# Upper products of an image as eight 64x32 tiles, and final products as four 64x64 tiles

## The chip, the cores and the metric

One core of one Trainium2 chip runs the kernel. The metric is the device time of one execution in microseconds. The five engines named below are TensorE (PE; its weight loads are listed as PEld), VectorE (DVE), ScalarE (ACT), GpSimd (POOL) and SyncE (SP), which only starts DMAs here.

## The reference, cut to what matters

The input x is 8 images of 64 channels on a grid of 16x16 points, fp32. Two layers follow each other, each with a group norm ahead of it and a residual sum behind it.

```python
x = x + local_attention(_gn(x), ...)        # 3x3 mean, q/k/v, 9 taps, 8 heads, gate, projection
x = x + relu(deformable_conv(_gn(x), ...))  # 64 -> 64 channels, 3x3 taps, 4 groups of 16 channels
```

The second layer takes most of the time. A 3x3 convolution gives for each point, tap (9) and group (4) an offset (dy, dx) and a mask. For each tap the image is sampled bilinearly at the shifted point, multiplied by the mask, and the 9x64 sampled values are multiplied by `w_dcn` and summed. A bilinear sample is a sum over rows and columns of the image, weighted by "hats" max(0, 1-|distance|) in y and in x. The kernel writes it as matrix products: weights made of image rows, times moving data made of the product of a y hat and an x hat. A weight matrix for one image and a pair of rows has 128 rows (2 image rows x 4 groups x 16 columns) and 64 columns (the channels), and is zero where the group of the row isn't the group of the channel.

## The kernel before

**Stages.** The attention layer runs until about 54 us. Then come the second norm, the offset convolution (`convolve`, in five pieces; pieces 3 and 4 are computed later, inside the sampling loop), the split of its results into three bf16 parts that go to `stack` by DMA, and from about 75 us the sampling loop `sampling(0)`. It has 72 steps: image i (0 to 7) and tap m (0 to 8). Every engine has its own order of work, written out by hand as a loop over the same steps, and semaphores tie the engines together. A second pass exists for far offsets (`it` not an int); it isn't run with these inputs.

**One step on TensorE** (`sampling` under `block.tensor`), in this order: `spread_y` of the next tap (6 matmuls of 256 columns, fp16, banks 0 to 3 in turn); on every second step `select_x` (4 matmuls, bank 5); a part of the products; a part of `convolve` in images 0 and 3; `select_y` (steps 1, 3, 7) and `spread_mask` (table `MASKS`), both to bank 7; `windows`; and in step `FINAL` the final products of the image before.

**The products.** PSUM holds for each image and each of three tap rows ki and two sides (halves of the image) a 64 x 384 block. The table `BLOCKS` puts two of them at a time in steps 6, 7 and 8, `LATE` in steps 0, 1 and 2 of the next image: kind 0 is ki 0 and 1 of side 0 in bank 4, kind 1 the same of side 1 in bank 6, kind 2 is ki 2 of both sides in bank 4. Each pair is two tiles of 128 rows x 64 columns. A tile takes up to 6 matmuls over row pairs, with 96, 192, 288, 288, 192, 96 moving columns; fp32 matmuls appear as two MATMUL records each. Kind 0 has no matmul for the row pair outside the image.

**One step on VectorE**: `multiply` (rows times x hat, PSUM to `smp`, L852); `values` (products times mask, L866) in steps 8, 1 and 3; `accumulate` and `finish` (L874, L879, L885) in step FINAL+1; then in this order `window_out` for odd window groups (L837), `offset_part` and `stage`.

**The windows.** `windows(g)` transposes four 128x128 blocks of image rows to PSUM (L1129, one record per transpose); ACT copies the even groups out, DVE the odd ones. There are 17 groups: three ahead of the loop, six in steps 0 to 5 of image 0, four each in steps 2 to 5 of images 1 and 2. Group g+1 waits for the copy of g where steps 3 and 5 say so.

**The final products** (`final`, in step 5 for the image before): 3 matmuls of 256 columns with `wa` and 6 of 128 columns with `wb`, all of 128 rows x 64 columns, into the two halves of bank 6. `accumulate` adds the two halves.

**At the start** ACT builds a permutation `by_tap`, PE multiplies it with the weights (`wfin`, L981 to L983), ACT copies pieces of the result to `wa` and `wb` (L495 to L502), and PE runs two filler products (`keep_warm(2)`, L976) before it multiplies q, k and v.

Of the kernel before, what the change touches and what calls it, by code (L numbers as in the profile page):

```python
# [5 lines left out]
B, C, H, W = 8, 64, 16, 16  # L6
HW = H * W
HALVES = 2
# [4 lines left out]
TAPS = 9  # L13
# [41 lines left out]
DX = DG * W  # L55

# [26 lines left out]
CHUNK, VALS, SLICES = 3, 3, 6  # L83
SEL_Y = {1: 0, 3: 1, 7: 2}
BLOCKS = {6: (0, 0), 7: (0, 1), 8: (1, 0)}
LATE = {0: (1, 1), 1: (2, 0), 2: (2, 1)}
FINAL = 5
# [7 lines left out]
def seventh(i, m):  # L95

    at = i * STEPS + m - 1
    while at >= 0:
        i, m = divmod(at, STEPS)
        if m in SEL_Y and i + 1 < B:  # L100
            return "y", 3 * (i + 1) + SEL_Y[m] + 1
        if m in MASKS[i]:
            c, part = MASKS[i][m]
            return "m", SLICES * c + part + 1
        at -= 1
    return "y", 3


def bass_local_attention_then_deformable_conv(nc, x, cf, wom, sel16, rows16, out):
# [8 lines left out]
    with ExitStack() as ctx:  # L118
# [24 lines left out]
        wa = sb("wa", [P, 3 * C])  # L143
        wb = sb("wb", [P, 6 * C])
# [119 lines left out]
        def mask_of(i, part):  # L264
# [3 lines left out]
            if part < 2:  # L268
                m = masks[:, at:at + 3 * BANK].rearrange("p (k i n) -> p k i n", k=3, i=2)[:, :, side_, part * HF:(part + 1) * HF]
# [9 lines left out]
        s_perm, s_wtap, s_wzero, s_wfin = sem("s_perm"), sem("s_wtap"), sem("s_wzero"), sem("s_wfin")  # L279
# [60 lines left out]
        def _(sp):  # L340
# [4 lines left out]
            sp.dma_start(selx[:, :].bitcast(u16), sel16["selx"]).then_inc(s_selxd, 16)  # L345
# [40 lines left out]
        def _(pool):  # L386
# [5 lines left out]
            nc.gpsimd.memset(wb[:, :], 0.0).then_inc(s_wzero, 1)  # L392
# [31 lines left out]
            pool.wait_ge(s_byd, 16)  # L424
            for a in range(2):
                src = bcast[:, 0:2 * DG * P].rearrange("p (d a r x) -> p a r d x", d=DG, a=2, r=WROWS)[:, a, 0:ROWS]
                dst = by_rows[:, a * QUARTERS * P:(a + 1) * QUARTERS * P].rearrange("p (r d x) -> p r d x", r=ROWS, d=DG)
                nc.gpsimd.tensor_copy(dst, src).then_inc(s_byrows, 1)
# [8 lines left out]
            def stage(j, shift):  # L437

                rows = images(tall)[:, j, bass.ds(shift * (ROWS * W), SROWS * W)].rearrange("p (r x) -> p r x", r=SROWS)
                nc.gpsimd.tensor_tensor(staged_image(j), rows.unsqueeze(2).to_broadcast([P, SROWS, DG, W]), group_mask(SROWS),  # L440
                                        ALU.mult).then_inc(s_staged, 1)
# [37 lines left out]
        def _(act):  # L479
# [9 lines left out]
            act.wait_ge(s_wzero, 1)  # L489
            lower, upper = slice(0, C), slice(C, P)  # L490
            straight = bank(1)[:, 0:PAIRS * C].rearrange("p (k o) -> p k o", o=C)
            swapped = bank(2)[:, 0:PAIRS * C].rearrange("p (k o) -> p k o", o=C)
            wa3 = wa[:, :].rearrange("p (k o) -> p k o", o=C)
            wb3 = wb[:, :].rearrange("p (k h o) -> p k h o", k=3, h=2)
            nc.scalar.copy(wa3[lower, 0:3:2], straight[lower, 0:2]).then_inc(s_wfin, 1)  # L495
            nc.scalar.copy(wa3[lower, 1], swapped[lower, 0]).then_inc(s_wfin, 1)
            nc.scalar.copy(wa3[upper, 0:3:2], straight[upper, 1:3]).then_inc(s_wfin, 1)
            nc.scalar.copy(wa3[upper, 1], swapped[upper, 2]).then_inc(s_wfin, 1)
            nc.scalar.copy(wb3[lower, 0:3:2, 0], straight[lower, 3:5]).then_inc(s_wfin, 1)
            nc.scalar.copy(wb3[lower, 1, 0], swapped[lower, 3]).then_inc(s_wfin, 1)  # L500
            nc.scalar.copy(wb3[upper, 0:3:2, 1], swapped[upper, 3:5]).then_inc(s_wfin, 1)
# [991 lines left out]
```

## Time and profile before

| what | value |
|---|---|
| median of 3 runs | 208.38 us (208.22 to 208.55) |
| the profiled execution's own time | 208.33 us |
| its span in the trace | 206.5 us |
| PE busy / DVE busy / ACT busy / POOL busy | 182.0 / 159.5 / 106.4 / 86.7 us |
| granted TensorE clock, mean | 0.999 |

The span is the time from the first to the last recorded instruction; the 1.8 us between it and the profiled time lie around it. A busy time is the union of an engine's instructions. PE records carry a modelled end which includes the way through the array, so starts of consecutive matmuls are a better measure than durations.

### The profile page before, as it was taken

The numbers are of one execution on the slowest core, as the hardware profiler recorded it, in microseconds if no ns is written. First come the engines' busy times: TensorE is split into PE (matmuls) and PEld (weight loads), VectorE is DVE, ScalarE is ACT, GpSimd is POOL, SyncE is SP. The second block draws the span as 40 slices with busy tenths as digits, with TensorE's granted clock in tenths as the row PEclk, the third lists the DMA queues.
The fourth block names the chain that finished last, engine by engine and source line by source line (L and its number), as shares of the span: only waits on it lengthen the run. The fifth ranks groups of instructions, "written<-read, shape, count | busy, mean of one in ns | idle before, by whom it ended". The sixth has DMA issues, their size and how long they took to land.

```text
span 206.5 us, 4572 instructions
## 1 busy us (share of the span) xinstructions
PE 182.0 (88%) x1808; PEld 127.9 (62%) x1808; DVE 159.5 (77%) x257; ACT 106.4 (51%) x199; POOL 86.7 (42%) x104
## 2 busy tenths in 40 slices
PE   0399996989989989999979999999969999998980
PEld 0224963644357535468668879639958789877870
DVE  0479958994869769888889779816999798899922
ACT  0325238500006795678748657836766687864000
POOL 8523982666013086504354343340561654442000
PEclk9999999999999999999999999999999999999999
DMA  6940000000040010010011000000002100000000
GB/s 193 325 28 0 3 0 2 3 0 0 0 102 14 25 30 9 17 43 3 7 29 33 0 3 0 3 0 0 12 25 62 28 0 16 2 16 2 19 0 21
DMA packets 8499, 5.54 MB, mean 27 GB/s; under 512 B 4887, under 2 KB 7461, under 8 KB 8473
## 3 DMA queue, kind: packets, MB, share of 16 engines
q1 hardware_dynamic: 8089, 4.25, 7.9%
q10 hardware_dynamic: 288, 0.89, 1.3%
q8 instruction: 16, 0.26, 0.5%
q14 instruction: 10, 0.08, 0.1%
q0 software_dynamic: 96, 0.06, 0.1%
HBM read 2.82 MB, written 0.52 MB: 16 GB/s over the span
## 4 chain that ended last, share of the span: by engine, by line
PE 67%; DVE 15%; ACT 6%; issue 4%; DMA 3%; POOL 2%; SPq 0%; DVEq 0%; ACTq 0%; POOLq 0%
PE ps L1218 20%; PE ps L1192 10%; PE ps L1112 10%; PE ps L1008 4%; PE ps L1129 3%; DVE smp_prod L742 3%; DMA x_parts<-in_x 3%; PE ps L1260 3%; PE ps L1266 3%; PE ps L1045 3%; PE ps L1177 2%; PE ps L991 2%; PE ps L1163 2%; DVE smp_prod L852 2%; PE ps L1146 2%
## 5 line engine op out<-in xcount | busy, mean ns | idle before, releaser
L852 DVE TENSOR_TENSOR smp_prod<-ps,hx_selx 128x768 f32<-128x768 f32 x72 | 67.5, 953 | 10.1 <-PE ps L1192 8.8
L1218 PE MATMUL ps<-smp_prod,windows_attention 128*64 128x192 f32 (+2 forms) x512 | 54.9, 336 | 0.0
L1218 PEld LDWEIGHTS ps<-smp_prod,windows_attention 128*64 128x64 f32 x512 | 40.1, 136 | 4.1 <-ACT windows_attention L574 0.3
L1192 PE MATMUL ps<-haty,by_rows 128*64 128x256 f16 x432 | 39.4, 275 | 2.0 <-DVE smp_prod L852 1.8
L450 POOL TENSOR_SCALAR disty<-disty 64x512 f32<-64x512 f32 (+1 forms) x23 | 13.5, 586 | 64.4 <-ACT haty L595 64.3
L1192 PEld LDWEIGHTS ps<-haty,by_rows 128*64 128x64 f16 x432 | 26.1, 109 | 9.7 <-DVE smp_prod L852 3.9
L603 ACT ACTIVATE hx_selx<-ps 128x512 f32<-128x512 f32 x36 | 21.3, 591 | 10.8 <-PE ps L1177 10.7
L457 POOL TENSOR_TENSOR haty<-disty,haty 64x512 f16<-64x512 f32 (+1 forms) x23 | 24.0, 1042 | 1.9
L1112 PE MATMUL ps<-conv_staged 128*108 128x512 f32 (+1 forms) x60 | 23.3, 521 | 0.7 <-ACT x_parts L567 0.7
L605 ACT ACTIVATE hx_selx<-hx_selx 128x512 f32<-128x512 f32 x36 | 22.7, 630 | 1.1
L590 ACT ACTIVATE disty<-ps 128x512 f32<-128x512 f32 (+1 forms) x24 | 12.5, 521 | 12.3 <-PE ps L1163 12.3
L581 ACT COPY windows_attention<-ps 128x512 f32<-128x512 f32 (+1 forms) x24 | 11.3, 473 | 10.7 <-PE ps L1146 9.5
L866 DVE TENSOR_TENSOR vals_attw<-ps,windows_attention 128x384 f32<-128x384 f32 x24 | 13.3, 554 | 4.1 <-PE ps L1218 3.4
L1177 PE MATMUL ps<-stack_x,selx 110*64 110x256 bf16 x144 | 15.6, 272 | 0.0
L453 POOL TENSOR_SCALAR disty<-disty 64x512 f32<-64x512 f32 (+1 forms) x23 | 14.8, 643 | 1.9
L1112 PEld LDWEIGHTS ps<-conv_staged 128*108 128x108 f32 x60 | 9.5, 172 | 8.0 <-issue 6.0
L595 ACT ACTIVATE haty<-disty 128x512 f16<-128x512 f32 (+1 forms) x24 | 13.4, 559 | 0.8
L567 ACT ACTIVATE x_parts<-ps,kept 108x256 f32<-108x256 f32 (+1 forms) x3 | 1.6, 540 | 22.1 <-PE ps L1112 22.0
L421 POOL TENSOR_TENSOR smp_prod<-smp_prod 128x1024 f32<-128x1024 f32 x4 | 9.3, 2358 | 6.0 <-DVE smp_prod L742 6.0
L1045 PE MATMUL ps<-smp_prod,kept 128*128 128x512 f32 x20 | 9.6, 611 | 1.6 <-POOL smp_prod L421 1.6
L742 DVE TENSOR_TENSOR smp_prod<-ps,windows_attention 128x1024 f32<-128x1024 f32 x9 | 10.5, 1212 | 0.1
L1163 PE MATMUL ps<-stack_y,s_sely 110*64 110x256 bf16 x80 | 9.4, 278 | 1.0 <-ACT windows_attention L581 0.7
(137 smaller groups left out, 273.9 us busy)
## 6 DMA issues: line engine op xcount, KB each, us to landing
x_parts<-in_x SPq DMA_DIRECT2D x2, 256.0 KB, 5.3
bcast<-in_bcast SPq DMA_DIRECT2D x2, 256.0 KB, 6.7
x2seq<-x_parts SPq DMA_DIRECT2D x2, 256.0 KB, 3.7
out<-x_parts SPq DMA_DIRECT2D x8, 64.0 KB, 2.2
vals_attw<-in_cf ACTq DMA_DIRECT2D x1, 480.0 KB, 5.8
stack_m<-x_parts SPq DMA_DIRECT2D x12, 36.0 KB
kept<-in_cf ACTq DMA_DIRECT2D x1, 390.5 KB, 4.5
conv_staged<-in_wom SPq DMA_DIRECT2D x1, 324.0 KB, 6.9
```

The costliest lines, as they stand in the source:

```text
L453: nc.gpsimd.tensor_scalar(d, d, -1.0, 1.0, ALU.add, ALU.mult).then_inc(s_uy, 1)
L457: nc.gpsimd.tensor_tensor(hi, d, hi, ALU.add).then_inc(s_loy, 1)
L603: nc.scalar.activation(h, bank(5), ACT.Abs).then_inc(s_absx, 1)
L605: nc.scalar.activation(h, h, ACT.Relu, bias=1.0, scale=-1.0).then_inc(s_hatx, 1)
L742: nc.vector.tensor_tensor(grid(prod[:, t * N:(t + 1) * N]), grid(bank(PB[pos % 3], 2)), shifted(vpad, t), ALU.mult).then_inc(s_pv, 1)
L852: nc.vector.tensor_tensor(pairs, rows, cols.unsqueeze(1).to_broadcast([P, QUARTERS, HW]), ALU.mult).then_inc(s_mult, 1)
L1045: ins = nc.tensor.matmul(bank(2 + c), ident, prod[:, t * N + c * BANK:][:, 0:BANK], start=(t == 0), stop=(t == 6))
L1112: ins = nc.tensor.matmul(bank(CONV_BANK[p])[0:OM, lo:hi], womt[:, k * OM:(k + 1) * OM], shifted(dup[h], 3 * ky + 2 * single)[:, j:j + (hi ...
L1163: ins = nc.tensor.matmul(bank(7)[h * C:(h + 1) * C, k * HW:(k + 1) * HW], sely[:, p * P + h * C:p * P + (h + 1) * C], stack["y"][:, i * HW ...
L1177: ins = nc.tensor.matmul(bank(5)[h * C:(h + 1) * C, k * HW:(k + 1) * HW], selx[:, tap * P + h * C:tap * P + (h + 1) * C], stack["x"][:, i ...
L1192: ins = nc.tensor.matmul(ps[h * C:(h + 1) * C, at:at + HW], by_matrix(a, QUARTERS - 1 - k)[:, h * C:(h + 1) * C], haty[i % 2][:, p * HW:(p ...
L1218: return nc.tensor.matmul(dst[:, at:at + strips * 3 * SP].rearrange("p (s k n) -> p s k n", k=3, n=SP), rows, sampled(i, ki, m, first, str ...
```

## The change

The 128 rows of the weights are put in another order, so that the first 64 partitions hold groups 0 and 1 and the last 64 groups 2 and 3 (e = 0, 1). A matrix for ki 0 or 1 then splits in two dense blocks of 64 rows x 32 columns. All eight (2 ki, 2 sides, 2 e) are issued interleaved, in steps 6 and 7 (`UPPER`), e = 0 to bank 4 and e = 1 to bank 6. Steps 8 and 0 have no products; ki 2 stays two tiles of 128x64, in steps 1 and 2 (`LOWER`). Masks of ki 0 and 1 come as eight 110x32 matmuls of 256 columns in place of two 110x64 of 512. Window transposes become eight matmuls of 128x64 with the identity. The final products become 18 matmuls of 64x64 and 128 columns, on four tiles, side 0 in bank 6 and side 1 in bank 7, and move from step 5 to step 4; `accumulate` moves from step 6 to 5. `values` part 1 moves from step 1 to 0. The x and y hats, staging and weights are laid out to match. Cut to its core:

```diff
-CHUNK, VALS, SLICES = 3, 3, 6
+CHUNK, VALS, SLICES = 2, 3, 6
-BLOCKS = {6: (0, 0), 7: (0, 1), 8: (1, 0)}
-LATE = {0: (1, 1), 1: (2, 0), 2: (2, 1)}
-FINAL = 5
+UPPER = {6: 0, 7: 1}
+LOWER = {1: 0, 2: 1}
+FINAL = 4
+EIGHTH = C // 2
...
-            sp.dma_start(selx[:, :].bitcast(u16), sel16["selx"]).then_inc(s_selxd, 16)
+            for r in range(2):
+                sp.dma_start(selx[:, :].bitcast(u16).rearrange("p (t e r c) -> p r t e c", t=TAPS, e=2, r=2)[:, r],
+                             sel16["selx"].rearrange("p (t r e c) -> p r t e c", t=TAPS, e=2, r=2)[:, r]).then_inc(s_selxd, 16)
...
-                    if (i, m) == (0, 6) and isinstance(it, int):
+                    if (i, m) == (0, 5) and isinstance(it, int):
                         offsets(3)
...
-                    if m == 1 and i:
+                    if m == 0 and i:
                         values(i - 1, 1, it)
...
-            nc.tensor.matmul(bank(1)[:, 0:PAIRS * C], by_tap[:, :], cst["wfin"], start=True, stop=True)
-            nc.tensor.matmul(bank(2)[0:C, 0:PAIRS * C], by_tap[:, C:P], cst["wfin"], start=True, stop=True)
-            nc.tensor.matmul(bank(2)[C:P, 0:PAIRS * C], by_tap[:, 0:C], cst["wfin"], start=True, stop=True).then_inc(s_wtap, 1)
+            for a in range(2):
+                for e in range(2):
+                    for u in range(4):
+                        nc.tensor.matmul(bank(1 + a)[u * EIGHTH:(u + 1) * EIGHTH, e * 3 * C:(e + 1) * 3 * C],
+                                         by_tap[:, a * C + e * EIGHTH:a * C + (e + 1) * EIGHTH], cst["wfin"][:, 0:3 * C],
+                                         start=True, stop=True)
+                for side in range(2):
+                    ins = nc.tensor.matmul(bank(0)[side * C:(side + 1) * C, a * 2 * C:(a + 1) * 2 * C],
+                                           by_tap[:, a * C:(a + 1) * C], cst["wfin"][:, 3 * C:5 * C], start=True, stop=True)
+            ins.then_inc(s_wtap, 1)
...
-                    ins = nc.tensor.transpose(bank(dst)[:, k * P:(k + 1) * P], rows, ident)
+                    for e in range(2):
...
+                        ins = nc.tensor.matmul(bank(dst)[e * C:(e + 1) * C, k * P:(k + 1) * P], rows, ident, start=True,
+                                               stop=True)
...
-                    for h in range(HALVES):
-                        ins = nc.tensor.matmul(bank(7)[h * C:(h + 1) * C], selm[:, k * P + h * C:k * P + (h + 1) * C], src,
-                                               start=True, stop=True)
+                    for e in range(2):
+                        for u in range(4):
+                            side, ki = divmod(u, 2)
+                            at = k * P + ki * C + e * EIGHTH
+                            ins = nc.tensor.matmul(bank(7)[u * EIGHTH:(u + 1) * EIGHTH, e * HW:(e + 1) * HW],
+                                                   selm[:, at:at + EIGHTH], sides[:, side], start=True, stop=True)
...
+            def upper_products(i, part, it):
+                if part == 0:
+                    reach(pe, s_mult, STEPS * i + 6, it)
+                    reach(pe, s_vals, VALS * i, it)
+                    reach(pe, s_acc, i, it)
+                    settled(pe, it)
+                products(i, [(ki, side, e, bank(6 if e else 4)[(2 * side + ki) * EIGHTH:(2 * side + ki + 1) * EIGHTH])
+                             for side in range(2) for ki in range(2) for e in range(2)], part, it)
...
             def final(i, it):
                 reach(pe, s_vals, VALS * (i + 1), it)
+                bank7_free(i + 1, FINAL if i + 1 < B else 0, it)
+                settled(pe, it)
+                def term(side, g, n, start, stop):
+                    rows = slice(side * C, (side + 1) * C)
+                    e, kj = divmod(n, 3)
+                    w = (wu[rows, n * C:(n + 1) * C] if e < 2 else wl[rows, kj * C:(kj + 1) * C])
+                    src = vals[rows, e * 6 * C:(e + 1) * 6 * C].rearrange("p (s k n) -> p k s n", k=3, n=SP)[:, kj]
+                    dst = bank(6 + side)[g * C:(g + 1) * C, 0:HF].rearrange("p (s n) -> p s n", n=SP)
+                    return nc.tensor.matmul(dst, w, src, start=start, stop=stop, skip_group_check=True)
+                for n in range(5):
+                    for side in range(2):
+                        if n < 4:
+                            term(side, 1, 5 + n, n == 0, n == 3)
+                        ins = term(side, 0, n, n == 0, n == 4)
+                ins.then_inc(s_fin, 1)
...
-                    if i == 0 and m < TAPSTEPS and isinstance(it, int):
+                    if i == 0 and m < 5 and isinstance(it, int):
                         if m == 0:
                             pe.wait_ge(s_omraw, 3)
-                        convolve(3, m)
+                        for n in (m,) if m < 4 else (4, 5):
+                            convolve(3, n)
```

Also in the diff: `stage` writes each image in two instructions (one per e) in place of one, `by_rows` is copied in four instructions in place of two, ACT makes 10 copies of the weights in place of 8, POOL no longer clears `wb`, `farthest` moves on DVE from step 4 to 3 of image 5, and PE waits for `s_omraw` 4 in step 6 of image 0 in place of 8.

## Rows read from the trace of the kernel before

**Rows 1.** The page: busy times, and the chain that ended last, by engine
```profile
PE 182.0 (88%) x1808; PEld 127.9 (62%) x1808; DVE 159.5 (77%) x257; ACT 106.4 (51%) x199; POOL 86.7 (42%) x104
PE 67%; DVE 15%; ACT 6%; issue 4%; DMA 3%; POOL 2%; SPq 0%; DVEq 0%; ACTq 0%; POOLq 0%
```
**Rows 2.** Busy time by stretch: stretch, length, PE, PEld, DVE, ACT, POOL, clock, DMA
```profile
76.00:90.20 14.20, 14.15 (x96) 6.92 (x96) 11.29 (x16) 8.67 (x16) 8.12 (x10) 1.00 0.07 19
90.20:99.20 9.00, 8.98 (x117) 7.00 (x117) 7.95 (x10) 7.80 (x15) 2.73 (x4) 1.00 0.04 11
...
106.80:116.30 9.50, 9.48 (x125) 8.05 (x121) 8.45 (x13) 6.79 (x13) 3.00 (x5) 1.00 0.09 26
...
123.10:133.30 10.20, 10.07 (x138) 8.53 (x133) 8.86 (x12) 7.89 (x16) 3.87 (x6) 1.00 0.01 2
...
141.30:155.40 14.10, 12.53 (x176) 10.97 (x173) 13.75 (x21) 9.34 (x18) 6.59 (x9) 1.00 0.06 16
155.40:168.10 12.70, 12.57 (x172) 10.44 (x170) 11.42 (x21) 9.50 (x18) 4.38 (x7) 1.00 0.13 34
...
180.80:192.90 12.10, 11.31 (x158) 9.72 (x155) 11.31 (x16) 6.03 (x10) 3.72 (x5) 1.00 0.03 8
```
**Rows 3.** Groups of instructions by line and form: busy us, mean ns
```profile
L852 DVE TENSOR_TENSOR smp_prod<-ps,hx_selx 128x768 f32<-128x768 f32 x72 | 67.5, 953 | 10.1 <-PE ps L1192 8.8 <-DVE x_parts L813 0.4
L866 DVE TENSOR_TENSOR vals_attw<-ps,windows_attention 128x384 f32<-128x384 f32 x24 | 13.3, 554 | 4.1 <-PE ps L1218 3.4 <-ACT windows_attention L581 0.5
```
**Rows 4.** Timeline of PE, one part of kind 2: start, length, what
```profile
171.21 1.19 PE L1218 MATMUL ps<-smp_prod,windows_attention 128*64 128x96 f32 x12
172.18 0.33 PE L1152 MATMUL ps<-stack_m,s_selm 110*64 110x256 bf16 x2
```
**Rows 5.** Attention logits, 32-column tiles: matmuls in flight in 20 ns; the chain
```profile
22.90:22.92 0.02, 0.02 (x4) 1.00 0.00 0
23.85:23.87 0.02, 0.02 (x8) 1.00 0.00 0
...
20.37 7.61 PE ps L1008 x144
```
**Rows 6.** Timeline of PE in image 0, step 1 to 2 of the loop
```profile
80.18 0.39 PE L1177 MATMUL ps<-stack_x,selx 110*64 110x256 bf16 x4
80.49 1.11 PE L1112 MATMUL ps<-conv_staged 128*108 128x512 f32 x2
81.44 0.60 PE L1129 MATMUL ps<-kept,smp_prod 128*128 128x128 f32 x4
81.97 0.52 PE L1192 MATMUL ps<-haty,by_rows 128*64 128x256 f16 x6
```
**Rows 7.** Timeline of PE at the start of the kernel
```profile
11.81 3.48 PE L976 MATMUL ps<-kept 128*128 128x512 f32 x4
15.70 1.10 PE L991 MATMUL ps<-windows_attention,vals_attw 128*128 128x512 f32 x2 [0.41 <-DVE windows_attention L703]
```
**Rows 8.** Timeline of ACT and PE ahead of the loop
```profile
71.37 0.60 ACT L590 ACTIVATE disty<-ps 128x512 f32<-128x512 f32 x1
...
76.04 1.11 PE L1112 MATMUL ps<-conv_staged 128*108 128x512 f32 x2 [0.67 <-ACT x_parts L567]
```
**Rows 9.** Timeline of image 2, steps 4 to 6
```profile
118.91 0.66 PE L1129 MATMUL ps<-kept,x_parts 128*128 128x128 f32 x4
...
119.68 0.68 DVE L837 COPY windows_attention<-ps 128x512 f32<-128x512 f32 x1
...
120.41 0.66 PE L1129 MATMUL ps<-kept,x_parts 128*128 128x128 f32 x4 [0.40 <-DVE windows_attention L837]
...
122.61 0.42 DVE L874 COPY x_parts<-ps 64x256 f32<-64x256 f32 x1 [1.38 <-PE ps L1266]
...
122.90 1.03 PE L1218 MATMUL ps<-smp_prod,windows_attention 128*64 128x192 f32 x8
```
**Rows 10.** Timeline of the last image
```profile
199.08 0.56 DVE L866 TENSOR_TENSOR vals_attw<-ps,windows_attention 128x384 f32<-128x384 f32 x1 [1.39 <-PE ps L1218]
199.69 0.86 PE L1260 MATMUL ps<-vals_attw,wa 128*64 128x256 f32 x5 [0.65 <-DVE vals_attw L866]
201.30 0.42 DVE L874 COPY x_parts<-ps 64x256 f32<-64x256 f32 x1 [1.66 <-PE ps L1266]
```

More of the change, by code:

```diff
@@ L488, in _ @@
             act.wait_ge(s_wtap, 1)
[L489 to L501, printed above, removed]
[L502 removed]
+            wu4 = wu[:, :].rearrange("p (e k o) -> p e k o", e=2, o=C)
+            wl3 = wl[:, :].rearrange("p (k o) -> p k o", o=C)
+            last = bank(0)[:, 0:4 * C].rearrange("p (a k o) -> p a k o", a=2, o=C)
+            for a in range(2):
+                taps = bank(1 + a)[:, 0:6 * C].rearrange("p (e k o) -> p e k o", e=2, o=C)
+                for side in range(2):
+                    for ki in range(2):
+                        rows = slice((2 * side + ki) * EIGHTH, (2 * side + ki + 1) * EIGHTH)
+                        if ki == a:
+                            nc.scalar.copy(wu4[rows, :, 0:3:2], taps[rows, :, a:a + 2]).then_inc(s_wfin, 1)
+                        else:
+                            nc.scalar.copy(wu4[rows, :, 1], taps[rows, :, 2 * ki]).then_inc(s_wfin, 1)
+            nc.scalar.copy(wl3[:, 0:3:2], last[:, 0]).then_inc(s_wfin, 1)
+            nc.scalar.copy(wl3[:, 1], last[:, 1, 0]).then_inc(s_wfin, 1)
             def out_of_q(c):
@@ L1224, in needed, with products @@
                         if not isinstance(it, int) or pair_of_rows(i, ki, m)[1]]
-            def products(i, tiles, dst, part, it):
-                lists = [needed(i, ki, side, it) for ki, side in tiles]
+            def products(i, tiles, part, it):
+                lists = [needed(i, ki, side, it) for ki, side, _, _ in tiles]
                 for m in range(part * 3, part * 3 + 3):
-                    for n, (ki, side) in enumerate(tiles):
+                    for n, (ki, side, e, dst) in enumerate(tiles):
@@ L1251, in final, with lower_products @@
+            def lower_products(i, part, it):
+                if part == 0:
+                    reach(pe, s_mult, STEPS * (i + 1), it)
+                    reach(pe, s_vals, VALS * i + 1, it)
+                products(i, [(2, side, None, bank(4)[side * C:(side + 1) * C]) for side in range(2)], part, it)
             def final(i, it):
                 reach(pe, s_vals, VALS * (i + 1), it)
-                both = vals[:, 0:12 * C].rearrange("p (s k n) -> p k s n", k=3, n=SP)
-                lower = vals[:, 12 * C:18 * C].rearrange("p (s k n) -> p k s n", k=3, n=SP)
@@ L1256, in final @@
-                out_ = [bank(6)[h * C:(h + 1) * C, 0:HW] for h in range(2)]
-                def upper(h, kj, start):
-                    return nc.tensor.matmul(out_[h].rearrange("p (s n) -> p s n", s=STRIPS), wa[:, kj * C:(kj + 1) * C],
-                                            both[:, kj], start=start, stop=False, skip_group_check=True)
-                def below(h, kj, top, stop=False):
-                    at = (2 * kj + top) * C
-                    return nc.tensor.matmul(out_[h][:, top * HF:(top + 1) * HF].rearrange("p (s n) -> p s n", n=SP),
-                                            wb[:, at:at + C], lower[:, kj], start=False, stop=stop, skip_group_check=True)
@@ L1335, in sampling @@
                         final(i - 1, it)
-                for m in range(3):
-                    block_of_products(B - 1, *LATE[m], it)
+                for part in range(2):
+                    lower_products(B - 1, part, it)
                 final(B - 1, it)
```

137 lines of the change are left out of this document (65 added, 72 removed).

## The prediction

> **What bounds the kernel now.** I read the page first, then the busy times by stretch, then timelines of one step each. On the page PE is the busiest engine and two thirds of the chain that ended last, with DVE second [rows 1]. That is an average over stages, so the table of stretches decides. The reader is to see three regimes in it [rows 2]. From 76 to 133 us, images 0 to 2, PE is busy for nearly the whole of each stretch shown (14.15 of 14.20, 8.98 of 9.00): time taken from or added to PE there moves the end. In image 3 to 4 (141.3 to 155.4) DVE has 13.75 of 14.10: a faster PE brings little. In the last images both are close: 12.57 PE and 11.42 DVE of 12.70, at the end 11.31 and 11.31 of 12.10. DVE's own work per image is 9 multiplies and 3 values, 9 x 0.953 + 3 x 0.554 = 10.2 us [rows 3], and about 1.3 for accumulate and finish (three of 0.42 to 0.5, one of them in rows 9). That is 11.6 us, a floor which the change doesn't touch.
>
> **Upper products.** Two tiles with 96+192+288 columns each, in two records per matmul (12 in all), take 172.18 - 171.21 = 0.97 us [rows 4], so a record costs 0.97/1152 = 0.84 ns per column with both tiles at once, at the granted clock of 1.00 (2.4 GHz). A full tile (1152 columns, two records) is 1.94 us, kind 0 with a strip less 1.77. The change puts kinds 0 and 1, 3.71 us, on eight tiles at once: 1.94 us if the array sets the pace. It issues 84 records. Eight tiles appear nowhere. The nearest rows are the 32-column tiles of the logits: 4 records are in flight with two tiles active and 8 where two calls with other tiles overlap [rows 5], so twice as many tiles do carry twice the work there, and the pace is 27 ns a record, half of 7.61/144 = 53 ns. 84 x 27 = 2.27 us. Bounds: 1.94 and 84 x 53 = 4.45. I take 2.1, near the row with most tiles: a gain of 1.6 us an image for PE.
>
> **Changes of tile shape.** Between a 64-column and a 128-column shape PE loses time: L1177 to L1112 is 0.31 us where two rounds of 256 bf16 columns take 0.21 (0.42 ns a column, half of fp32's); L1112 to L1129 is 0.95 for 2 x 512 x 0.84 = 0.86, by a first weight load of 128 columns; L1129 to L1192 is 0.53 for four transposes that need 0.44 [rows 6]. So about 0.1 us lies in each gap, and some more in the first weight load behind it: I use 0.12 towards the narrower shape, 0.18 towards 128 columns. The change brings new ones: four an image for the upper products (two where a mask follows joins them), two for final, two for each mask slice of ki 0 and 1, some nine in all, or 1.1 us an image. The Trainium skill, "TensorEngine Tiling (Array Packing)", Key Properties, says that a change of tiling mode, not of tile, drains TensorE, which speaks against this change; by that rule the price applies to all nine, and rows 6 agree for the one pair that they show. Bounds from rows: 0 (a kind not shown) and 0.18.
>
> **Windows.** Four transposes are 0.44 us [rows 6]. Eight fp32 matmuls of 128 columns on two tiles are 16 records x 128 x 0.84/2 = 0.86: +0.42 each, 17 times. Where no convolution stands beside them the two changes to 128 columns (0.30) go, which leaves +0.12.
>
> **The sum, by place.** The list adds to the profiled execution's 208.33 us, which is the median's within 0.05.
> 1. Start. The weight products grow from 6 records of 320 columns to 24. They run at half rate: four records of 512 columns take 3.48 [rows 7], 0.85 each against 0.43 (512 x 0.84) later. Four rounds of 192 columns (0.32 each) and two of 128 (0.21), twice, with four changes, end some 1.4 us later than now. Fillers follow and end near 15.3; q/k/v wait until 15.70 for DVE, so 0.4 of it is hidden, and part of the fillers falls into the full clock. +0.15.
> 2. Ahead of the loop, windows 0 and 1 stand before the select_y which ACT awaits at 71.37; from there ACT is busy without a gap to 75.99, and PE waits for it until 76.04 [rows 8]. Two times 0.42 and some of a change: +0.95. ACT hid nothing there.
> 3. Image 0, steps 0 to 5, PE-bound [rows 2]: +0.42 in steps 0 and 2, +0.12 in 1 and 3, +0.24 in 4, +0.06 in 5, where a convolution piece leaves and takes its two changes with it: +1.4.
> 4. Products of images 0, 1, 2 (90.2 to 133.3, three stretches of rows 2): -1.6 each, +0.48 for their changes, +0.12, 0.6, 0.24 for masks, less about 0.2 idle that goes. DVE's 7.95 of 9.00 is the next limit in the first. -0.9 -0.7 -0.75 = -2.35.
> 5. Steps 4 to 6 of images 1 and 2. Window group 16 waits for DVE's copy of 15, which now follows multiply 5 at once [rows 9]. After the change final stands in step 4 and accumulate and finish in step 5 ahead of that copy, so the chain is window 15 (0.86), final (1.25), accumulate and finish (1.35 with the way to DVE), copy (0.68), window 16 (0.86), ACT's copy (0.6, so far beside final), upper. From window 15 at 118.91 to the product at 122.90 are 4.0 us now; the chain has 5.6 and some 0.3 of waits and a change, and window groups 13 and 14 add 0.8 before it. +2.6; in image 1 DVE has other work there which already held PE: +1.8. What queues behind PE's wait is spread_y for tap 7, so DVE waits as well.
> 6. Image 3 to 4, DVE-bound; accumulate and finish now fall in the convolution gap ahead: -0.5.
> 7. Images 4 to 6 (37.5 us): upper part 0 starts when accumulate is done; DVE then has finish, multiplies 6, 7, 8 (3.3 us) against PE's two parts, changes and spread_y (3.3). So DVE is the bound, 11.6 and 0.2 of gaps each, +0.3 for farthest in image 5: 35.7. -1.8.
> 8. End. From values part 2 to accumulate 1.66 [rows 10] becomes 1.5, and lower products start at values part 0: -0.3.
> Sum: 0.15 + 0.95 + 1.4 - 2.35 + 4.4 - 0.5 - 1.8 - 0.3 = +1.95, so **210.3 us**. The rest costs nothing by its cover: the split DMA of selx (needed at 68 us, all loads of constants are done by 15), four copies on POOL for two (POOL waits 8.7 us behind them), ACT's weight copies (needed by 20 us), two stage instructions for one (+0.1, DVE waits there).
>
> **Rivals.** (B) Faster: the new shape changes cost nothing, since only 64 to 128 columns is shown. Against: it is the same engine and the same gap. Nine an image in stretches 4 (-2.0), two in step 5 (-0.5), the end and item 1 (-0.6), and 8-tile products at 1.94 (-0.4): 206.8. It decides below about 0.06 us a change. If the copy chain of item 5 also costs half, 205.
> (C) Eight tiles don't pay: records go no faster than 53 ns over a long run [rows 5], 4.45 us an image, 2.35 above my value in all eight: PE is then the bound everywhere, 210.3 + 8 x 2.1 = 227; at 40 ns, 3.4 us, about 216. For: no row has row tiles. Against: 8 in flight. The Trainium skill, "TensorE: Matmul & The Clock Gate", Part 1, names some 62 ns per MATMUL without hardware decode; by an estimate from that page 84 would take 5.2 us, but rows 4 and 5 show shorter paces in bursts, so I give it little.
> (D) PE gains but DVE and ACT are late everywhere, no net change: 208.4.
>
> **Chances.** Forecast 0.50, C 0.11, B 0.33, D 0.06. Less than 0.2% (0.42 us) can't be told from no change here. Slower 0.61, same 0.06, faster 0.33. The range 205.2 to 214.8 holds B with half of the chain, and C only up to some 35 ns a record; the forecast's own range is 208.8 to 212.5 (change price 0.08 to 0.15, chain 3 to 5).
>
> **What would show it.** Upper records: 40 in step 6, spanning 1.0 to 1.1 us start to start (right), 2 or more (C). Gaps at upper and final of about 0.1 beyond column time (B: none). L1129's successor: 0.86 per group. The wait of PE for L837 in images 1 and 2: over 2 us each against 0.40 now. L852's idle in the last images near zero, period 11.8. Wrong if the loop starts no later than now or if windows aren't 0.4 longer.

## The result: 220.2 us, 5.6% slower

| | before | after |
|---|---|---|
| median (lowest to highest, 4 runs each) | 208.36 us (208.22 to 208.55) | 220.21 us (219.81 to 220.47) |
| span of the profiled execution | 206.5 us | 217.9 us |
| instructions of PE (matmuls) | 1808 | 2598 |

The ratio is 1.056, 95% interval 1.055 to 1.058. Forecast were 210.3 us and a range of 205.2 to 214.8: slower was right, but of +11.85 us only +1.95 had been seen. Two executions among the experiments (222.45 us in the fourth, 223.56 us in the ninth) were over 1.5% longer than the fastest of their kernel, and the medians and ratios given there leave them out. The page of after, which answers to [rows 1]:

```profile
PE 181.0 (83%) x2598; PEld 117.7 (54%) x2598; DVE 162.2 (74%) x261; ACT 108.1 (50%) x201; POOL 84.9 (39%) x105
PE 55%; DVE 21%; ACT 9%; issue 8%; DMA 3%; POOL 2%; DVEq 0%; SPq 0%; ACTq 0%; POOLq 0%
```

PE works 1.0 us less and the kernel takes 11.4 us more, and the chain that ended last holds less PE and more DVE, ACT and issue. The time lies in waits. To see where, I cut both kernels at the first multiply of each image; the last stretch reaches to the end. Columns as in [rows 2]: stretch, length, PE, PEld, DVE, ACT, POOL, clock, DMA. Before:

```profile
71.92:93.46 21.54, 20.86 (x162) 11.11 (x164) 17.98 (x23) 15.84 (x30) 11.23 (x12) 1.00 0.09 24
...
126.17:144.59 18.42, 18.29 (x189) 12.69 (x187) 11.23 (x16) 12.12 (x23) 6.25 (x9) 1.00 0.00 1
...
158.95:171.62 12.67, 12.54 (x170) 10.46 (x168) 11.39 (x21) 10.05 (x19) 6.52 (x9) 1.00 0.10 24
...
sum 134.58, PE 123.06 PEld 94.19 DVE 106.79 ACT 83.00 POOL 52.24; mean PE 15.38 PEld 11.77 DVE 13.35 ACT 10.38 POOL 6.53
```

After:

```profile
72.42:97.15 24.73, 23.32 (x324) 14.15 (x320) 18.66 (x24) 16.01 (x30) 10.17 (x12) 1.00 0.08 21
97.15:116.55 19.40, 15.48 (x304) 11.81 (x300) 14.93 (x22) 11.71 (x23) 6.23 (x9) 1.00 0.05 15
116.55:134.65 18.10, 15.63 (x310) 11.95 (x310) 12.56 (x17) 10.72 (x21) 6.25 (x9) 1.00 0.03 7
134.65:154.48 19.83, 17.86 (x264) 10.16 (x260) 11.37 (x15) 12.39 (x23) 6.23 (x9) 1.00 0.01 2
154.48:169.45 14.97, 11.84 (x232) 8.30 (x234) 14.71 (x21) 8.84 (x18) 6.82 (x9) 1.00 0.10 28
169.45:184.12 14.67, 12.62 (x252) 8.21 (x248) 12.15 (x19) 10.61 (x20) 6.24 (x9) 1.00 0.08 20
184.12:197.58 13.46, 11.47 (x232) 8.47 (x234) 11.75 (x16) 8.74 (x18) 6.25 (x9) 1.00 0.03 8
197.58:217.90 20.32, 12.83 (x260) 9.31 (x256) 13.09 (x20) 4.35 (x8) 2.39 (x3) 0.91 0.05 11
sum 145.48, PE 121.04 PEld 82.35 DVE 109.21 ACT 83.38 POOL 50.56; mean PE 15.13 PEld 10.29 DVE 13.65 ACT 10.42 POOL 6.32
```

The reader is to take the length less PE's busy time: over the loop it grows from 134.58 - 123.06 = 11.5 us to 145.48 - 121.04 = 24.4. Image 3 had 0.13 us of it and has 1.97, image 5 had 0.13 and has 2.05. No engine is full in images 1, 2, 3, 5 and 6. The table sets the lengths beside the prediction's sum; its items 6 and 7 go by places half an image or more later than these stretches, so its terms are regrouped and the last three rows match only roughly.

| stretch | before | after | change | forecast (items) |
|---|---|---|---|---|
| up to the first multiply | 71.92 | 72.42 | +0.50 | +1.10 (1, 2) |
| image 0 | 21.54 | 24.73 | +3.19 | +0.50 (3, part of 4) |
| image 1 | 17.51 | 19.40 | +1.89 | +1.10 (4, 5) |
| image 2 | 15.20 | 18.10 | +2.90 | +1.85 (4, 5) |
| image 3 | 18.42 | 19.83 | +1.41 | -0.50 (6) |
| images 4 to 6 | 40.13 | 43.10 | +2.97 | -1.80 (7) |
| last image | 21.80 | 20.32 | -1.48 | -0.30 (8) |

The place that item 7 spoke of, image 6, steps 4 to 6, in the timeline of after (start, length, what, idle before it):

```profile
189.25 2.04 DVE L867 TENSOR_TENSOR smp_prod<-ps,hx_selx 128x768 f32<-128x768 f32 x2
...
190.74 0.45 PE L1298 MATMUL ps<-vals_attw,wu 64*64 64x128 f32 x8 [0.23 <-ACT disty L603]
...
192.10 0.42 DVE L888 COPY x_parts<-ps 64x256 f32<-64x256 f32 x1 [0.82 <-PE ps L1298]
192.55 0.43 DVE L893 TENSOR_TENSOR x_parts<-ps,x_parts 64x256 f32<-64x256 f32 x1
193.01 1.17 DVE L899 SCALAR_TENSOR_TENSOR x_parts<-x_parts,x2seq 64x256 f32<-64x256 f32 x1
194.21 2.69 DVE L867 TENSOR_TENSOR smp_prod<-ps,hx_selx 128x768 f32<-128x768 f32 x3
```

Multiplies 4 and 5 run, then DVE waits 0.82 us for final, does accumulate (L888, L893) and finish (L899), and only then multiply 6. Before, the same place reads:

```profile
177.56 2.90 DVE L852 TENSOR_TENSOR smp_prod<-ps,hx_selx 128x768 f32<-128x768 f32 x3
...
178.98 0.81 PE L1260 MATMUL ps<-vals_attw,wa 128*64 128x256 f32 x5
...
180.54 0.42 DVE L874 COPY x_parts<-ps 64x256 f32<-64x256 f32 x1
```

Three multiplies in a row run beside final, and accumulate follows 0.08 us behind them. The forecast had moved accumulate one step ahead at no cost.

### The profile page after: what moved, and what is told of

It is laid out like the page before. It is cut to its first block, busy times and chain, and to the rows that moved or that the text cites. A ratio compares the mean times of both kernels' runs of the same rounds, so it can differ in the third digit from the quotient of the medians.

```text
span 217.9 us, 6167 instructions
## 1 busy us (share of the span) xinstructions
PE 181.0 (83%) x2598; PEld 117.7 (54%) x2598; DVE 162.2 (74%) x261; ACT 108.1 (50%) x201; POOL 84.9 (39%) x105
## 4 chain that ended last, share of the span: by engine, by line
PE 55%; DVE 21%; ACT 9%; issue 8%; DMA 3%; POOL 2%; DVEq 0%; SPq 0%; ACTq 0%; POOLq 0%
PE ps L1249 12%; PE ps L1133 9%; PE ps L1151 6%; PE ps L1219 6%; DVE smp_prod L867 4%; PE ps L1298 4%; PE ps L1029 3%; DVE smp_prod L755 3%; ACT disty L603 3%; DMA x_parts<-in_x 3%; PE ps L1066 3%; PE ps L1190 2%; PE ps L1012 2%; PE ps L1204 2%; DVE x_parts L893 1%
## 5 line engine op out<-in xcount | busy, mean ns | idle before, releaser
L463 POOL TENSOR_SCALAR disty<-disty 64x512 f32<-64x512 f32 (+1 forms) x23 | 13.1, 569 | 80.3 <-ACT haty L608 80.2
L1219 PE MATMUL ps<-haty,by_rows 128*64 128x256 f16 x432 | 36.6, 275 | 4.9 <-DVE smp_prod L867 4.9
L1249 PE MATMUL ps<-smp_prod,windows_attention 64*32 64x192 f32 (+5 forms) x848 | 37.1, 337 | 3.0 <-ACT windows_attention L587 1.1
L1249 PEld LDWEIGHTS ps<-smp_prod,windows_attention 64*32 64x32 f32 (+1 forms) x848 | 23.7, 112 | 10.9 <-issue 3.3
L1219 PEld LDWEIGHTS ps<-haty,by_rows 128*64 128x64 f16 x432 | 22.3, 109 | 13.2 <-DVE smp_prod L867 9.3
L1204 PE MATMUL ps<-stack_x,selx 110*64 110x256 bf16 x144 | 14.3, 273 | 0.0
L466 POOL TENSOR_SCALAR disty<-disty 64x512 f32<-64x512 f32 (+1 forms) x23 | 13.5, 588 | 1.9
L1298 PE MATMUL ps<-vals_attw,wu 64*64 64x128 f32 x192 | 10.6, 277 | 2.4 <-ACT disty L603 1.4
L1298 PEld LDWEIGHTS ps<-vals_attw,wu 64*64 64x64 f32 x192 | 8.7, 132 | 4.7 <-issue 2.8
```

Of the source, the lines that this page charges most:

```text
L466: nc.gpsimd.tensor_scalar(d, d, -1.0, 1.0, ALU.add, ALU.mult).then_inc(s_uy, 1)
L1204: ins = nc.tensor.matmul(bank(5)[h * C:(h + 1) * C, k * HW:(k + 1) * HW], selx[:, tap * P + h * C:tap * P + (h + 1) * C], stack["x"][:, i ...
L1219: ins = nc.tensor.matmul(ps[h * C:(h + 1) * C, at:at + HW], by_matrix(a, QUARTERS - 1 - k)[:, h * C:(h + 1) * C], haty[i % 2][:, p * HW:(p ...
L1249: return nc.tensor.matmul(dst[:, at:at + strips * 3 * SP].rearrange("p (s k n) -> p s k n", k=3, n=SP), rows, sampled(i, ki, m, first, str ...
L1298: return nc.tensor.matmul(dst, w, src, start=start, stop=stop, skip_group_check=True)
```

## Experiments

W is the theory that the loss is waits, that is the order of the work; S that the narrow shapes (windows, changes of shape) cost more than rated. The kernel before was timed beside each group of runs: 208.5 to 208.6 us. After was timed once, for the result above: 220.2 us. The code is shortened to the lines that matter.

**The windows alone, in the kernel before.**

```diff
-ins = nc.tensor.transpose(bank(dst)[:, k * P:(k + 1) * P], rows, ident)
+for e in range(2):
+    ins = nc.tensor.matmul(bank(dst)[e * C:(e + 1) * C, k * P:(k + 1) * P], rows[:, e * C:(e + 1) * C],
+                           ident, start=True, stop=True)
```

> The kernel before with one edit: each of the four transposes of a window group becomes two fp32 matmuls of 64 columns (the form that the change brings), same partition order, same values. It prices the windows alone. Theory W (the 11.85 us are waits: PE work that used to stand between the users of bank 7 and between final and the next multiply is gone) expects only the terms of the prediction: two groups ahead of the loop +0.84, seven in image 0 +1.4, eight in images 1 and 2 at +0.12 to 0.42, so about +3.5, 211.9 us. Theory S (the narrow shapes and their changes cost more than rated) expects at least half of the missing 9.9 us here: 215 us or more.

212.56 us, ratio 1.019 (1.013 to 1.024): +4.0. By stretch, from the trace: the first multiply comes 1.07 us later (forecast for the two groups ahead of the loop: 0.95), image 0 is 1.60 longer (1.4), image 1 0.42, image 2 1.15, and the rest is unchanged to 0.06. W is borne out against S: the windows cost 4.0 us where 3.5 had been expected.

**The windows taken back, in the changed kernel.**

```diff
-for e in range(2):
...
-    ins = nc.tensor.matmul(bank(dst)[e * C:(e + 1) * C, k * P:(k + 1) * P], rows, ident, start=True,
-                           stop=True)
+ins = nc.tensor.transpose(bank(dst)[:, k * P:(k + 1) * P], rows, ident)
```

> The changed kernel with the windows as four whole 128x128 transposes a group, as before. Their rows then lie in another order in the image of windows, so the sampled values are wrong; the rest of the work is the same. Theory W: the mirror of the first run, about -3.5 of 220.2, so 216.7 us. Theory S: -7 or more, 213 us or less.

218.55 us, ratio 1.044 (1.037 to 1.052), lowest run 216.54: -1.7 in the median, less than either theory said. By stretch, image 0 gives back 2.15 us, but image 1 is 1.05 longer than in after. In images 1 and 2 the granted clock was 0.92 and 0.91 in the mean, where after has 1.00:

```profile
94.46:114.91 20.45, 16.05 (x256) 10.89 (x252) 14.93 (x23) 11.82 (x23) 6.23 (x9) 0.92 0.05 15
114.91:133.14 18.23, 16.03 (x262) 10.59 (x262) 12.56 (x17) 10.58 (x21) 6.26 (x9) 0.91 0.02 6
```

By these rows the clock cost up to 0.08 x 20.45 + 0.09 x 18.23 = 3.3 us. With 1.7 that is 5.0, near what the windows cost (4.0 in the kernel before, 4.8 by the run with both causes undone, below). They are not S's cause, and there is a second effect, the clock, taken up below.

**The order.** Final back in step 5, accumulate behind multiply 6, upper products in steps 7 and 8, mask slice of step 6 in step 4.

```diff
-UPPER = {6: 0, 7: 1}
+UPPER = {7: 0, 8: 1}
-FINAL = 4
+FINAL = 5
-         {0: (1, 2), 2: (1, 3), 6: (1, 4), 8: (1, 5)}, {0: (2, 0), 2: (2, 1), 6: (2, 2), 8: (2, 3)},
+         {0: (1, 2), 2: (1, 3), 4: (1, 4), 8: (1, 5)}, {0: (2, 0), 2: (2, 1), 4: (2, 2), 8: (2, 3)},
...
-                    if m == 8:
-                        values(i, 0, it)
                     if m == 0 and i:
+                        values(i - 1, 0, it)
+                    if m == 1 and i:
                         values(i - 1, 1, it)
```

> The changed kernel, same instructions, other steps: final back in step 5 (behind spread_y for tap 6, so that multiply 6 can run beside it) with accumulate behind multiply 6, the upper products in steps 7 and 8, values part 0 and 1 in steps 0 and 1, the mask slice of step 6 in step 4. Theory W: the 5.3 us from multiply 5 to 7 of images 5 and 6 (3.1 and 3.9 before) shorten by some 1.5 an image, and so do those of images 1 to 3; 220.2 - 7 = 213 us. Theory S: the order changes nothing much, 219 to 221 us.

212.13 us, ratio 1.017 (1.011 to 1.024): 8.1 us less than after with the same instructions. This is the main finding. By stretch against after: -0.78 in image 0, -1.98, -1.83, -1.50, -0.93, -0.81 and -1.12 in images 1 to 6, +1.02 at the end. Two rows of its stretches:

```profile
130.17:148.50 18.33, 17.73 (x273) 10.33 (x278) 11.17 (x17) 12.38 (x23) 6.24 (x9) 1.00 0.01 2
...
176.41:188.74 12.33, 11.26 (x240) 8.20 (x229) 11.63 (x17) 9.51 (x19) 6.25 (x9) 1.00 0.04 9
```

In these two PE's busy time is that of after to 0.2 us; what went is idle (image 3: 1.97 to 0.60, image 6: 1.99 to 1.07), and image 6 is now held by DVE, 11.63 of 12.33, 0.8 shorter than before, which is the kind of gain that item 7 had forecast.

**DVE's copies ahead of accumulate.**

```diff
+                    if isinstance(it, int):
+                        if (i, m - 1) in PAIRS_AT:
+                            g, src = PAIRS_AT[i, m - 1]
+                            if g % 2:
+                                window_out(g, it, src)
                     if m == FINAL + 1 and i:
                         accumulate(i - 1, it)
```

> The changed kernel with DVE's copies of window groups in front of accumulate and finish. Only images 1 and 2 have both in step 5. The prediction's item 5 has accumulate and finish (1.35 us and ways) in front of the copy that window groups 12 and 16 wait for; with the copy first it runs beside final, and the first upper product of those images comes some 2.0 us sooner: 220.2 - 3.5 = 216.7 us. If the upper products are held by accumulate anyway (they wait for it too), it is 0.7 us later there and nothing is won: 220 to 221 us.

218.07 us, ratio 1.042 (1.034 to 1.050), lowest run 216.70. Image 1 is 1.43 shorter than in after and image 2 1.92, 3.35 together as expected: the chain of item 5 is real. But in the profiled execution image 3 is 1.7 longer. The trace says why (columns as above, the clock is the last but two):

```profile
132.00:134.00 2.00, 0.63 (x8) 0.36 (x8) 1.97 (x3) 1.97 (x4) 1.21 (x2) 1.00 0.00 0
134.00:136.00 2.00, 1.92 (x24) 1.57 (x26) 0.79 (x1) 0.97 (x3) 1.17 (x2) 0.64 0.00 0
136.00:138.00 2.00, 2.00 (x16) 1.27 (x14) 0.17 (x1) 1.09 (x3) 0.00 (x0) 0.51 0.00 0
138.00:140.00 2.00, 2.00 (x32) 1.35 (x28) 1.51 (x2) 0.98 (x3) 1.15 (x3) 1.00 0.00 0
```

PE had little to do from 132 to 134 and was then granted half its clock (1.2 GHz) for some 3.5 us of full work: 0.36 x 2 + 0.49 x 2 = 1.7 us lost. So a gap in PE can cost more than its length. But it is no new gap that did it. PE's wait ahead of the fall, in this run and then the same wait in after:

```profile
134.08 0.40 PE L1174 MATMUL ps<-stack_m,s_selm 110*32 110x256 bf16 x8 [1.44 <-ACT windows_attention L594]
```

```profile
137.04 0.40 PE L1173 MATMUL ps<-stack_m,s_selm 110*32 110x256 bf16 x8 [1.44 <-ACT windows_attention L594]
```

In after the clock stayed at 1.00 behind it, and behind longer ones (1.48 and 1.70 us) too. In the loop of after the clock is 1.00 in seven stretches; the 0.91 of the last one holds its end, where PE has no work left (0.64 from 213 us on).

**Mask slices on 32-column tiles, in the kernel before.**

```diff
-                    for h in range(HALVES):
...
+                    for half in range(2):
+                        for u in range(4):
```

> The kernel before with each mask slice of ki 0 and 1 (twelve slices, two matmuls of 64x512 columns) written as eight matmuls of 32 output columns and 256 columns, same values: the same column time on the array and two more changes of tile shape a slice. It prices the change of shape, of which the prediction put 0.12 us on each. Nine of the twelve slices lie in images 0 to 3, which PE bounds: +2.1 us by the prediction's price, 210.5; by rival B (shape changes free) 208.4. By theory S (more than rated) 0.25 us a change or more: 213.

Two matmuls of 64 columns by 512 become eight of 32 by 256. 210.43 us, ratio 1.008 (1.004 to 1.013). In step 6 of image 0 the PE timeline of this kernel reads

```profile
90.28 1.03 PE L1221 MATMUL ps<-smp_prod,windows_attention 128*64 128x192 f32 x8
91.24 0.40 PE L1148 MATMUL ps<-stack_m,s_selm 110*32 110x256 bf16 x8
91.57 0.52 PE L1195 MATMUL ps<-haty,by_rows 128*64 128x256 f16 x6
```

From the products to spread_y are 91.57 - 90.28 = 1.29 us, against 91.25 - 90.17 = 1.08 in before (the starts of L1218 and L1192 there): 0.21 for two changes, 0.11 each where 0.12 was taken. Rival B is out. The total near the 210.5 forecast is in part luck: images 0 and 1 became only 0.12 us longer with five slices in them, where the price gives 1.2, and images 4 to 6, left out of the expectation, 0.91. In steps 4 and 5 of image 0 the slice stands between a convolution piece and window transposes, so it has a change on either side in before too: from it to the transposes are 0.34 us there and 0.33 here, and nothing is added. The Trainium skill, "TensorEngine Tiling (Array Packing)", Key Properties, has it that a change of tiling mode drains TensorE; the trace agrees, at 0.11 us a change.

**Finish behind multiply 6.**

```diff
                         accumulate(i - 1, it)
-                        if isinstance(it, int):
+                    if isinstance(it, int):
+                        if m == FINAL + 2 and i:
                             finish(i - 1, 1)
```

> The changed kernel with finish moved behind multiply 6 (step 6), accumulate as it is. In the trace finish stands between accumulate and multiply 6, 0.42 us long, 1.16 in images 5 and 6. If multiply 6 is what the image waits for there (theory W), the copy for groups 12 and 16 and multiply 6 come 0.4 us sooner in images 1 to 4 and 1.2 in 5 and 6: 220.2 - 3.5 = 216.7. If finish only moves and is paid a step later (DVE is the bound), -1 at most: 219.2 or more.

218.33 us, ratio 1.046 (1.039 to 1.053), and its profiled span is 2.5 us shorter than after's: 0.44, 0.45, 0, 0.09, 0.78, 0.93 in images 1 to 6. Between the two expectations; finish was in the way, most where it took 1.16 us, and some is paid a step later.

**Only final in step 5; only the products in 7 and 8.** The two halves of the third run, each alone (the mask slice moves with final).

> The changed kernel with final in step 5, accumulate behind multiply 6 and the mask slice of step 6 in step 4, but the upper products still in steps 6 and 7: one half of the third run. Multiply 6 then runs beside final, but the upper products still wait for accumulate in the step in which it ends, as they hold both banks. Theory W, first half (multiply behind accumulate costs): two thirds of the 8 us, 215 us. W, second half (the products' place costs): PE now waits for accumulate in front of the products, and most of it stays: 218 to 221 us.

221.03 us, ratio 1.056 (1.049 to 1.063).

> The other half of the third run: the changed kernel with the upper products in steps 7 and 8 (values part 0 and 1 in steps 0 and 1 of the next image), but final in step 4 and accumulate and finish ahead of multiply 6 as in the change. The half with final alone won nothing (221.0). If the two halves only work together (the products must not wait for accumulate, and multiply 6 must not wait for final), this half brings under 2 us: 218.5 to 220.5. If the products' place alone was the loss, it brings the 8 us: 212.5.

220.89 us, ratio 1.056 (1.049 to 1.063). Neither half wins anything, both together 8 us. With final alone moved, images 1, 2 and 6 are 1.08, 0.98 and 0.97 shorter than in after, but 3 and 4 are 1.97 and 1.69 longer, where its clock was 0.92 and 0.90:

```profile
133.00:135.00 2.00, 0.65 (x10) 0.36 (x8) 2.00 (x3) 1.94 (x5) 1.06 (x2) 1.00 0.00 0
135.00:137.00 2.00, 1.77 (x28) 1.40 (x30) 1.00 (x2) 1.39 (x4) 1.32 (x2) 0.82 0.00 0
137.00:139.00 2.00, 2.00 (x16) 1.37 (x14) 0.08 (x1) 1.20 (x3) 0.00 (x0) 0.50 0.00 0
```

With the products alone moved, images 0 to 3 are 0.79, 1.54, 0.62 and 1.51 shorter, and 5, 6 and the last 2.4, 1.4 and 2.6 longer, at clocks of 0.90, 0.94 and 0.95. Each half does win in most images where the clock held, and a fall of the clock takes that back (0.10 x 17.1 = 1.7 us of the 2.4 in image 5). With the products alone moved, PE's gaps ahead of the falls are longer than in after (1.79 and 2.16 us); with final alone moved, the first fall follows the same gap of 1.44 us that stands in after. That the halves work only together is so of the times, and the clock is a large part of why; how much of the 8 us each half is worth at a full clock was not measured.

**Upper products over three steps.**

```diff
-UPPER = {6: 0, 7: 1}        # window rows 0-2, 3-5
+UPPER = {6: 0, 7: 1, 8: 2}  # window rows 0-1, 2-3, 4-5
```

> The changed kernel with the same 84 records of upper products over steps 6, 7 and 8 (two window rows each) where the change has 6 and 7. Theory W in the form that PE work must stand between the users of bank 7: 2 us less, 218. If only the place of the start counts (bank 6 and accumulate), no gain, or values part 0 comes later: 220 to 221.

223.55 us, ratio 1.071 (1.066 to 1.076): 3.3 us slower. My form of W by which PE lacked work between the users of bank 7 is wrong. Values part 0 need the last window row, which now comes a step later: in image 5 DVE waits 1.59 us in front of them, where after has 0.27.

**The eighth run's edits.** On the third run's order, finish behind multiply 7 and ACT's reads of bank 7 ahead of its hats; and the same two edits on the kernel before.

```diff
-if t % 2 == 0 and t // 2 + LEAD < UNITS: hat_x(...)
 if m in SEL_Y and i + 1 < B: distance_y(...)
 if m in MASKS[i]: mask_out(...)
+if t % 2 == 0 and t // 2 + LEAD < UNITS: hat_x(...)
```

> The third run's order and two edits more: finish behind multiply 7, and ACT reads bank 7 (distance, masks) ahead of its hats of a step. In the third run PE waits 0.2 to 1.1 us an image for these reads, 1.1 in image 0. Theory W: -1.5, 210.6 us. If DVE bounds the images already: -0.3, 211.8.

210.59 us, ratio 1.009 (1.006 to 1.013): -1.5.

> The kernel before with the two edits that the eighth run added: finish one step later, ACT's reads of bank 7 ahead of its hats. A control: before has PE work beside these reads. Theory W: under 0.6 us less, 208.0 against 208.5; if they help it as much as the third run's order (-1.5), the edits say nothing of the change.

211.04 us, ratio 1.011 (1.007 to 1.016): 2.5 us slower, where -0.6 was expected. The trace has image 1 1.35 and image 5 1.22 longer. In the old order those edits hurt, so an order is good only for its own durations; I followed this no further.

**Last image in the change's own order, a mask slice of image 5 later.**

> The eighth run's kernel with two edits: the last image keeps the change's own steps (final in 4, upper products in 6 and 7, values part 0 in 8), whose end was 1.5 us shorter than before's where the eighth run's was 0.6 shorter; and the mask slice that stands between select_y and final in step 4 of image 5, where PE waits 1.1 us for ACT, goes to steps 8 and later. 210.6 - 0.9 - 1.0 = 208.7, level with before. If image 5 is held by DVE: 209.7.

210.88 us, ratio 1.010 (1.005 to 1.015): nothing won. Image 5 is 0.80 shorter than in the eighth run and image 6 1.13 longer, the end 0.26 shorter. No version that keeps the windows in the order which the changed products need beat the kernel before.

**Both causes undone.** The third run's order with the second run's whole windows.

> The third run's order (212.1 us) with the window groups as whole 128x128 transposes (as in the second run the rows then lie in another order, so sampled values are wrong). If order and windows are two separate causes, their sum: 212.1 less the 4.0 us of the first run = 208.1, which is the time before. If the waits take back what the windows give, as in the second run (1.7 of 4.0): 210.4.

207.37 us, ratio 0.993 (0.990 to 0.997). Order and windows are two separate causes: the windows give 212.13 - 207.37 = 4.8 us on top of the order, somewhat more than the 4.0 of the first run. So the 11.85 us are 8.1 for the order and 4.8 for the windows, less some 1 us that the rest of the change wins, its narrow masks (1.9 us in the fifth run) already paid; against 208.58 us, the time before beside this run, it is 1.2. Narrow masks and the final products on four tiles weren't taken back by themselves in the changed kernel. It isn't a version to use, as the window rows lie in the wrong order; whether the new order can be had with whole transposes wasn't tried.

**Tile by tile.**

```diff
-for m in range(part * 3, part * 3 + 3):
-    for n, (ki, side, e, dst) in enumerate(tiles):
+for n, (ki, side, e, dst) in enumerate(tiles):
+    for m in range(part * 3, part * 3 + 3):
```

> The changed kernel with the upper products' loops swapped: all window rows of one 64x32 tile, then the next tile, in place of one row on all eight tiles. Same records, same columns. If eight tiles run together only where neighbours in the queue are on different tiles, a record goes by its own columns (some 190 x 0.42 to 0.84 ns), 84 records 6.7 to 13 us an image against 2.3, and the kernel takes 250 to 290 us. If the array takes records of one tile as fast (27 ns each), the time stays at 220.

251.66 us, ratio 1.204 (1.198 to 1.211). The two parts of image 0 in this kernel's timeline:

```profile
93.62 2.04 PE L1249 MATMUL ps<-smp_prod,windows_attention 64*32 64x192 f32 x40 [0.77 <-ACT windows_attention L587]
...
96.38 4.10 PE L1249 MATMUL ps<-smp_prod,windows_attention 64*32 64x288 f32 x44
```

and the first of them in after:

```profile
93.36 1.18 PE L1249 MATMUL ps<-smp_prod,windows_attention 64*32 64x96 f32 x40 [0.77 <-ACT windows_attention L587]
94.47 0.40 PE L1173 MATMUL ps<-stack_m,s_selm 110*32 110x256 bf16 x8
```

In after 40 records take 94.47 - 93.36 = 1.11 us, and 44 take 1.12 on its chain: 2.23 us for 84, 27 ns a record on average. Tile by tile they are 2.04 + 4.10 = 6.1. The 3.9 more, eight times, are 31.2 us and the median is 31.4 longer; that these agree so well is luck, as the single images of this kernel are 3.0 to 5.8 us longer. The expectation had each record go by its own columns, 6.7 us or more. The 84 records have 17280 columns, by estimate 14.5 us at 0.84 ns if one followed another, so some tiles still ran together; and the second part took twice the first for 5% more columns, which is open.

## Why the prediction was wrong, and where it was right

- **Upper products: right.** 2.23 us against 2.1 taken; 84 records at 27 ns had given 2.27. The pace is set by the columns, though: in after eight records of 288 columns come 0.24 us behind the eight before them, and eight of 192 columns 0.16 us (288 and 192 x 0.84 ns), 20 ns a record. Rival C is out. 40 records in step 6 spanned 1.11 us, as written.
- **Price of a change of shape: right** (0.11 against 0.12). From its first matmul to the next instruction of PE final takes 1.25 us in after, 1.30 to 1.35 before.
- **Windows (items 2 and 3): right.** +1.07 ahead of the loop, +1.60 in image 0 by the first run, 4.0 us in all; in the changed kernel 4.8. The start (item 1) lost nothing that could be seen: q/k/v begin at 15.26 us in after, 15.70 before [rows 7], the input having landed 0.43 sooner in that execution, and that is why the loop begins only 0.50 later.
- **Copy chain (item 5): right in size.** After's chain of waits in image 2:

```profile
125.02 0.88 PE ps L1151 x16
125.90 1.27 PE ps L1298 x36
127.19 0.43 DVE x_parts L888
127.64 0.44 DVE x_parts L893
128.55 0.70 DVE windows_attention L852
129.30 1.12 PE ps L1151 x16
130.44 0.59 ACT windows_attention L587
131.08 1.18 PE ps L1249 x36
```

  From window group 15 to the upper product are 131.08 - 125.02 = 6.06 us, against 5.9 forecast and 4.0 before [rows 9]. The fourth run got 3.35 of the 4.4 us back.
- **Item 7 failed, and with it 6 and 4.** "DVE is the bound, 11.6 and 0.2 of gaps each": DVE is busy for 12.15 of 14.67 us in image 5 and 11.75 of 13.46 in image 6, so the gaps are 2.5 and 1.7. The step rated the work between accumulate and the next image (3.3 us on either engine) but not the way to it: final in step 4 stands in PE's queue ahead of spread_y for tap 6, and accumulate in step 5 stands in DVE's ahead of multiply 6. So multiply 6 waits for final, accumulate and finish, one behind the other, and all upper products wait for accumulate as they fill banks 4 and 6 together. Images 4 to 6 missed the forecast by 4.8 us. Items 6 and 4 rest on the same belief that 1.6 us less of PE work an image reach the end; image 3 missed by 1.9, image 0 by 2.7. The order as a whole is 8.1 us by the third run, which took back final's step, accumulate's, the products' and that of one mask slice.
- **In image 0** there is no final. Of its 3.19 us whole windows give back 2.15 (second run) and the products' place 0.78 (third run); with both undone it is 0.27 longer than before. Within it PE idles 0.77 us ahead of the first product. The profile names ACT's copy of group 8, but that had ended at 92.67; the product, at 93.36, also needs multiply 5, which ends just then:

```profile
91.40 1.96 DVE L867 TENSOR_TENSOR smp_prod<-ps,hx_selx 128x768 f32<-128x768 f32 x2
```

- **A term mis-sized: finish.** It was put at 0.42 to 0.5 from the last image. In images 5 and 6 of after it takes 1.16 and 1.17, and in image 6 of before already 1.04, which the mean of 0.50 us there had hidden. DVE's floor of 11.6 was too low there.
- **The end (item 8)** was better than thought, -1.48 against -0.3. On the chain of waits of before the last products are one run of 4.83 us ahead of values part 2 (199.08); in after there are 4.1 us from the second part of the eight-tile products to that values part:

```profile
206.85 1.19 PE ps L1249 x44
208.06 0.57 DVE vals_attw L881
208.76 2.15 PE ps L1249 x22
210.94 0.57 DVE vals_attw L881
```

  This is where PE's gain does reach the end, some 0.8 us; the item had counted only that the lower products start earlier.
- **By its own tests:** PE's wait for the copy was to exceed 2 us in images 1 and 2, and the longest were 1.5 and 1.7; the period of the last images was to be 11.8, and is 14.97, 14.67 and 13.46.

## What to carry to other kernels

A change that makes one engine's work shorter is priced by what stands ahead of the next instruction in every queue that it moves past, not by busy times: here the faster products were real (3.7 to 2.2 us), and moving final, accumulate, the products and a mask slice to other steps cost 8.1 us. Where two accumulators are filled at once, both have to be free at once; look at who holds each before gathering work. And when a rewrite changes durations, try the order again before judging it: the same instructions in other steps were 8 us faster.

## What the runs showed of the hardware

- Eight fp32 tiles of 64x32 run together when neighbours in the queue lie on different tiles: 2.23 us for 84 records, 27 ns each. With the same records queued tile by tile they overlap less: 2.04 us for 40 and 4.10 us for 44, 51 and 93 ns each.
- Finish, a DVE instruction with two operands in SBUF, doesn't end while GpSimd works on a tensor_tensor that began first. The row of POOL beside the one of 193.01 above:

```profile
192.74 1.16 POOL L470 TENSOR_TENSOR haty<-disty,haty 64x512 f16<-64x512 f32 x1
```

  It ends at 193.90; finish takes 1.17 us from 193.01, ending 0.28 behind it, where its usual 0.42 would have ended at 193.43. Of eight finishes, both that began inside such an instruction were long in after, and the one of before. The Trainium skill, "SBUF — State Buffer", SBUF: two separate sides, says that the pair of ports shared by the two is locked for a whole instruction by whoever starts first; these rows agree. Accumulate, which reads PSUM, was never long: in after both of its instructions began inside such a tensor_tensor (108.24 to 109.39, L888 at 108.65, L893 at 109.11) and took 0.42 us each.
- The clock: after a stretch of 2 us in which PE was busy for 0.63 or 0.65, the granted clock fell to 0.5 for some 3 us of full work and came back, which cost 1.7 us each time. It took back part of what an edit had won in four of these runs. It doesn't follow every gap: in the second run PE was busy for 0.52 of the 2 us from 108 us on, and the clock stayed at 1.00; and the wait of 1.44 us that a fall followed in the fourth run had none behind it in after. When it falls stays open.
